# Attention and ternary feed-forward in float32 on one core: the feed-forward joins the block of projections and attention

## What is computed

```python
x = x + attention(layernorm(x))       # causal; q, k from latents, half of each head rotated
x = x + ffn(layernorm(x))

def ternary_quant(w):
    scale = mean(abs(w)) + 1e-8
    return clip(round(w / scale), -1, 1) * scale

up, gate = h @ wu.T, h @ wg.T          # 512 -> 2048
hidden = silu(up) * gate
return hidden @ wd.T                   # 2048 -> 512
```

## Time and profile before

| | |
|---|---|
| time, median of 3 runs | 1896.14 us (1895.67 to 1896.91) |
| the profiled execution | 1895.38 us, span 1893.6 us, mean TensorE clock 0.992 |
| TensorE (PE) busy | 1834.3 us, 97%, 10898 matmuls |
| VectorE (DVE) busy | 1337.8 us, 71% |
| ScalarE (ACT) busy | 1036.3 us, 55% |
| GpSimd (POOL) busy | 521.9 us, 28% |
| DMA | 153.31 MB, mean 81 GB/s |

### The profile page before, as it was taken

One profiled execution on the slowest core, in us unless ns is written; L12 is line 12 of the kernel. 1 busy time (PEld: TensorE's weight loads), 2 busy tenths in 40 slices (PEclk: granted clock), 3 DMA queues, 4 the chain that ended last, 5 costly groups with the idle time before them and its releaser, 6 DMA issues. The chain is left out here.

```text
span 1893.6 us, 30946 instructions
## 1 busy us (share of the span) xinstructions
PE 1834.3 (97%) x10898; PEld 1602.4 (85%) x10898; DVE 1337.8 (71%) x2818; ACT 1036.3 (55%) x2485; POOL 521.9 (28%) x314
## 2 busy tenths in 40 slices
PE   6899988999999999999999999999999799999998
PEld 4788876899999999999999999999999677777777
DVE  5466657888888888888888888888888633333333
ACT  2223326786777766676666666676666332223232
POOL 4466652120120154253244235234323000000000
PEclk9999999999999999999999999999999899999999
DMA  3399996422232121221221221212111150000000
GB/s 120 113 226 226 224 234 176 129 73 77 65 94 62 50 80 62 62 62 62 68 62 62 58 65 52 73 40 68 40 57 39 58 210 1 22 0 22 15 7 22
DMA packets 96625, 153.31 MB, mean 81 GB/s; under 512 B 12528, under 2 KB 46448, under 8 KB 96240
## 3 DMA queue, kind: packets, MB, share of 16 engines
q1 hardware_dynamic: 84976, 130.66, 23.5%
q10 hardware_dynamic: 11520, 20.98, 4.2%
HBM read 97.06 MB, written 54.53 MB: 80 GB/s over the span
## 5 line engine op out<-in xcount | busy, mean ns | idle before, releaser
L1140 ACT CAST turned_hi<-ps_turn 128x512 fp32r<-128x512 f32 (+1 forms) x576 | 312.8, 570 | 257.2 <-PE ps_turn L1325 253.3
L1096 ACT ACTIVATE probs<-ps_scores,bias 128x512 f32<-128x512 f32 (+3 forms) x640 | 401.0, 639 | 71.1 <-DVE bias L1184 70.9
L1223 DVE TENSOR_TENSOR turned_lo<-ps_turn,turned_hi 128x512 fp32r<-128x512 f32 (+1 forms) x576 | 375.0, 656 | 60.7 <-ACT turned_hi L1140 55.4
L1325 PE MATMUL ps_turn<-ident,probs 128*128 128x128 f32 x2176 | 300.9, 272 | 1.4 <-DVE turned_lo L1223 1.1
L1181 DVE TENSOR_REDUCE negmax<-ps_scores 128x1 f32<-128x512 f32 (+1 forms) x384 | 257.4, 675 | 44.9 <-PE ps_scores L1284 39.6
L1325 PEld LDWEIGHTS ps_turn<-ident,probs 128*128 128x128 f32 x2176 | 255.4, 140 | 33.5 <-issue 2.2
L1026 POOL TENSOR_TENSOR q_lo<-q_raw,q_hi 128x512 fp32r<-128x512 f32 x64 | 82.8, 1294 | 677.0 <-ACT q_hi L1088 677.0
L1284 PE MATMUL ps_scores<-k_hi,q_hi 128*128 128x512 f32 (+2 forms) x576 | 231.0, 401 | 4.5 <-ACT probs L1096 4.4
L1344 PE MATMUL ps_o<-turned_hi,kv_hi 128*128 128x256 f32 x1088 | 226.7, 285 | 0.0
L1344 PE MATMUL ps_o<-turned_lo,kv_hi 128*128 128x256 f32 x1088 | 223.6, 282 | 0.0
L1344 PE MATMUL ps_o<-turned_hi,kv_lo 128*128 128x256 f32 x1088 | 223.4, 282 | 0.0
(11 more groups left out here) (152 smaller groups left out, 3502.8 us busy)
## 6 DMA issues: line engine op xcount, KB each, us to landing
plainT<-plain_out ACTq DMA_DIRECT2D x64, 256.0 KB, 4.0
rotT<-rot_out SPq DMA_DIRECT2D x64, 256.0 KB, 4.3
all_signs<-signs SPq DMA_DIRECT2D x24, 512.0 KB, 2.8
q_raw<-plainT SPq DMA_DIRECT2D x128, 64.0 KB, 2.4
q_raw<-rotT SPq DMA_DIRECT2D x256, 32.0 KB, 2.1
signs<-in_W_up SPq DMA_DIRECT2D x16, 512.0 KB, 3.6
signs<-in_W_gate SPq DMA_DIRECT2D x16, 512.0 KB, 3.7
signs<-in_W_down SPq DMA_DIRECT2D x16, 512.0 KB, 3.6
```

The source lines that it names most:

```text
L1096: nc.scalar.activation(probs_of(n, i)[:, h, first_key:first_key + keys], ps_scores[:, pieces.number[args] % RING, 0:keys], ACT.Exp, scale= ...
L1140: nc.scalar.copy(turned[0][:, at, cols(*args)], ps_turn[:, bank, cols(*args)]).then_inc(turned_hi_ready, 1)
L1223: nc.vector.tensor_tensor(turned[1][:, at, cols(*args)], ps_turn[:, bank, cols(*args)], turned[0][:, at, cols(*args)].bitcast(F32), ALU.su ...
L1325: last = nc.tensor.transpose(ps_turn[:, bank, (2 * b + h) * P:(2 * b + h + 1) * P], probs_of(n, i)[:, h, key:key + P], ident[:])
```

## The change

One block now holds projections, attention and feed-forward; `feed_forward` gives each engine's part as functions. Its code is written out, with no loop: 64 steps over (chunk, step), `down` a step late across chunks, up two steps ahead at the start, and no normalising in the last chunk. Its buffers lie over those that the attention has done with (`places`), its PSUM banks are ps_scores (up, gate, turns) and ps_turn and ps_o (sums). y holds the tiles in the order of the slots (15, 0, 14, 1, ...), so that the first chunk of the feed-forward is complete after two slots of the last pass; x is loaded tile by tile, 16 DMAs in place of 4.

In the last pass `Plan` has new events: the statistics at steps 40 to 49, the root at 64, normalising, transposes and splits of the first chunk from 64.4 on, and the weights' loads at 55 (4 tiles) and 66 (11 tiles; 9 more follow in the feed-forward). Behind the last pass up and gate of the first steps lie between the last output products.

In `last_order` the EARLY stages lie one piece later or earlier; the key splits go head by head, those of the second head's low parts to GpSimd.

```diff
@@ last_order @@
-    order += [(EARLY, 1), (ROT, 0, 1), (EARLY, 2), (PLAIN, 0, 0), (PLAIN, 0, 1), (EARLY, 3)]
-    order += [(ROT, 1, 1), (EARLY, 4), (PLAIN, 1, 0), (PLAIN, 1, 1)]
-    order += [(ROT, 2, 1), (PLAIN, 2, 0), (PLAIN, 2, 1), (EARLY, 5)]
-    return order + [(ROT, 3, 1), (PLAIN, 3, 0), (PLAIN, 3, 1)]
+    order += [(EARLY, 1), (ROT, 0, 1), (PLAIN, 0, 0), (PLAIN, 0, 1), (EARLY, 2)]
+    order += [(ROT, 1, 1), (PLAIN, 1, 0), (PLAIN, 1, 1), (EARLY, 3)]
+    order += [(ROT, 2, 1), (PLAIN, 2, 0), (PLAIN, 2, 1), (EARLY, 4)]
+    return order + [(ROT, 3, 1), (PLAIN, 3, 0), (PLAIN, 3, 1), (EARLY, 5)]
@@ Plan @@
-        self.only[0] += [(12, 0, "load_y", (2,)), (16, 0, "load_y", (1,))]
+        self.only[0] += [(4 + 12 * m, 0, "load_y", (m + 1,)) for m in range(NC - 1)]
...
+        last += [(40 + 3 * t, 0, "ln_stats", (t,)) for t in range(TC)] + [(53, 0, "ln_var", ()), (64, 0, "ln_root", ())]
...
+        last += [(55, 0, "load_ffn", (0,)), (66, 0, "load_ffn", (1,))]
...
@@ early_scalar @@
+        if stage == 2:
+
+            split_hi(act, 0, "split_q", (0,), 0)
             act.wait_ge(first_loaded, 48)
...
+            first_high(act, 0, 0)
+            first_high(act, 0, 1)
         if stage == 3:
...
+            for h, c in ((0, 2), (0, 3), (1, 0), (1, 1)):
+                first_high(act, h, c)
+        if stage == 4:
+            first_high(act, 1, 2)
+            first_high(act, 1, 3)
             split_hi(act, 0, "split_q", (1,), 0)
@@ early_gpsimd @@
+        if stage == 2:
+            split_lo(pool, 0, "split_q", (0,), 1)
+        if stage == 3:
+            low(1, 0)
+        if stage == 4:
+            low(1, 1)
+            low(1, 2)
+            low(1, 3)
+        if stage == 5:
+            split_lo(pool, 0, "split_q", (1,), 2)
@@ early_vector @@
-        if stage in (2, 4):
-            for c in (stage - 2, stage - 1):
-                for h in range(2):
-                    raw, hi, lo = first_views(c, h)
-                    dve.wait_ge(first_hi_ready, 2 * c + h + 1)
-                    nc.vector.tensor_tensor(lo, raw, hi.bitcast(F32), ALU.subtract).then_inc(first_ready, 1)
...
+        if stage in (3, 4):
+            for c in (2 * stage - 6, 2 * stage - 5):
+                raw, hi, lo = first_low(dve, 0, c)
+                nc.vector.tensor_tensor(lo, raw, hi, ALU.subtract).then_inc(first_ready[0], 1)
@@ attention, tensor @@
+                if kind in TAIL:
+                    if (kind, *args) == ("h_turn", 0):
+
+                        pe.wait_ge(exp_done, RING + softened.upto(last_of_all, 0))
+                    tail["tensor"](pe, kind, *args)
@@ feed_forward @@
+    def tensor(pe):
+        down(pe, 0)
+        for n, i, e in steps():
+            if n > AHEAD:
+                into_hidden(pe, n, UP)
+            into_hidden(pe, n, GATE)
+            down(pe, n - 1)
+            if i + 1 < NC and e in NORM_AT:
+                turn(pe, i + 1, NORM_AT[e])
+        down(pe, NC * ET - 1)
```

More of the change, by code:

```diff
@@ L643 @@
 NSLOTS = len(SLOTS)
+TILES = [t for tiles in SLOTS for t in tiles]
 CHUNKS = len(MATS) * PAIRS
@@ new lines, in down @@
+    def down(pe, n):
+        i, e = divmod(n, ET)
+        pe.wait_ge(hid_lo_ready, n + 1)
+        for t in range(TC):
+            if e == 0 and i:
+                pe.wait_ge(result_ready, TC * (i - 1) + t + 1)
+            if n == 0 and t == TC - 1:
+                pe.wait_ge(*keep["outs_over"])
+            for part in range(2):
+                last = nc.tensor.matmul(ps_acc[t], hid[part][:, n % 2, t * P:(t + 1) * P],
+                                        wT[DOWN][e // 2][:, e % 2, :], start=(e == 0 and part == 0),
+                                        stop=(e == ET - 1 and part == 1))
+            if e == ET - 1:
+                last.then_inc(acc_ready, 1)
@@ new lines, in sync, with scalar @@
+    def sync(sp):
+        sp.wait_ge(gate_ready, AHEAD + 1)
+        for c in range(5, PAIRS):
+            for m in (UP, GATE, DOWN):
+                load_weights(sp, m, c)
+        for i in range(NC):
+            for t in range(TC):
+                sp.wait_ge(result_ready, TC * i + t + 1)
+                sp.dma_start(out.rearrange("(t p) d -> t p d", p=P)[TILES[TC * i + t], :, :],
+                             result[:, t, :]).then_inc(stored[t], 16)
+    def scalar(act):
+        for n, i, e in steps():
+            silu(act, n)
+            hidden_high(act, n)
+            if i + 1 < NC:
+                if e == ROOT_AT:
+                    root(act, i + 1)
+                if e in NORM_AT:
+                    h_high(act, i + 1, NORM_AT[e])
@@ L1751, in _ @@
                     att["tensor"](pe)
[L1752 removed]
+                    ffn["tensor"](pe)
 def by_unit(name, w):
```

490 lines of the change are left out of this document (250 added, 240 removed).

## The result

| | |
|---|---|
| after, median of 4 runs | 1862.47 us (1857.74 to 1865.71) |
| before, median of 4 runs beside it | 1895.91 us (1893.55 to 1896.91) |
| ratio | 0.9822, 95% interval 0.9808 to 0.9836 |
| profiled execution after | 1864.14 us, span 1862.3 us |
| forecast | 1872.0, range 1864.5 to 1880.0 |

The change is faster, as forecast, but by 33.4 us instead of 24. The profiled run itself was 31.2 us faster than the one of before.

A forecast was written before the change was run, and what follows sets the result against it. TensorE was taken to set the pace in the attention, with holes at two seams and feed-forward stalls. -4.4 + 0.5 + 2.1 + 2.3 - 18.1 - 4.2 - 1.8 = -23.6 from 1895.4 gave 1872 us, range 1864.5 to 1880.

The forecast's parts named there:

- First seam: Projections to attention: reordered key splits and scores start the first exponentials earlier, -4.4 us, bounds -7.5 and 0.
- The slip of 1.5 us: First seam: two plain stores running against the query loads delay the queries' landing by 0 to 2.1 us, taken as 1.5.
- The rival: First seam: the reorder gives nothing, from delayed queries and engines locking each other out; 1876, at most 1878 us; chance 0.12.
- The lock of VectorE and GpSimd: First seam: the engines fully block each other, two splits held up 1.15 us each; the part gives -2.1, not -4.4.
- Statistics, transposes, normalising in the last pass: Last attention pass: added statistics +0.5, 16 transposes +2.1, root and normalising of the first chunk +2.3 us.
- the dearer price of a switch: Last pass, ScalarE's root: table switch of 1.28 us plus a drain of 1.38 more, making the +2.3 part +3.7.
- The rival of VectorE as the bound: Last pass: 3.5 us of statistics and 4.9 of normalising both come through, 1879 us; chance 0.10.
- Second seam: Attention to feed-forward: up and gate fill the hole, 11.4 us against 29.5 from the last value product, -18.1 us.
- Feed-forward without a loop: Feed-forward: down a step late across chunks removes six stalls of 0.70 us, -4.2; turning no unused chunk, -1.8.
- the unused turns: Feed-forward: the loop's fourth round turned a following chunk for nobody; dropping its 16 transposes gives -1.8 us.
- My sign for "wrong": Feed-forward in the changed profile: starts more than 0.2335 us apart would show the forecast wrong.
- Slower because the written-out code isn't fed: Unrolled feed-forward: some 2,300 more instructions, 6 more instruction-queue packets at 5.0 us each, 30 us, 1902; chance 0.03.

The follow-up runs named there:

- e1: Kernel before with only the new order at the first seam (last_order, key and query splits, scores one piece earlier): 1892.12 us against 1895.15, ratio 0.9982.
- e5: Kernel before with 32 bytes of padding ahead of hT, leaving the feed-forward's operands 192 apart modulo 256: 1895.42 us, ratio 0.9994.
- e9: Kernel before with hT, hidden and result 96 bytes further, so feed-forward operands start at the same place modulo 256: 1885.24 us, ratio 0.9957.
- e10: Kernel before with hT, hidden and result 224 bytes further, operands 128 apart modulo 256: 1895.16 us, ratio 0.9997.
- e3: Kernel before with the feed-forward's PSUM banks placed as in the changed kernel, nothing else moved: 1897.63 us, ratio 1.0010.
- e2: Kernel before with only TensorE's feed-forward loop written out: 1896.06 us, ratio 1.0005.
- e6: Kernel before with wT moved 32 bytes further instead of hT, operands 192 apart modulo 256: 1895.66 us, ratio 0.9996.
- e13: Kernel before with all matmul operands padded to 128 modulo 256: 1882.53 us, ratio 0.9931.
- e12: Changed kernel with the last down product of each chunk back inside its chunk: 1865.00 us, ratio to before 0.9853.
- e8: Changed kernel with gated, hidden and its two parts 32 bytes further, so only the down product is out of step: 1863.42 us, ratio to before 0.9825.
- e14: Changed kernel with 96 bytes of padding ahead of all tiles behind the scales, all operands at 128 modulo 256: 1856.71 us, ratio to before 0.9800.

## Why the prediction was right or wrong

**First seam: right in size, not in shape.** -4.4 stood against -4.59 in the traces and -4.95 in the means. I had one hole of 6 us near 282, and the trace of the changed kernel has 1.94 and 1.29 and then two waits on VectorE's splits. The slip of 1.5 us that I gave the queries didn't come. They were there 10.89 us behind the last wvo product before and 10.05 after, 1.72 us after ScalarE was ready for them, and so the bank was free earlier than in my walk. The first exponentials gained more than I said (21.80 us behind the wvo product instead of 28.37), and 2 us of that were gone at the fifth output product. ScalarE's wait of 2.55 us for the second head's maxima lies between; that it took them is argued, not shown. The granted clock fell to 0.50 at this seam too, for 6.8 us before and 3.4 after, in the other profiles for 10.2 to 13.7 with the old order and 0 to 6.8 with the new; the walk had no price for it, and how much of the gain it is wasn't told apart. That the size came out is in part luck. The rival fell with e1 and the stretches beside it.

The lock of VectorE and GpSimd, which I had priced at 2.3 us, is there in full:

```profile
287.47 3.04 DVE L1235 TENSOR_TENSOR k_lo<-first_raw,k_hi 128x512 fp32r<-128x512 f32 x2 [3.79 <-ACT k_hi L1065]
...
292.75 0.92 DVE L1235 TENSOR_TENSOR k_lo<-first_raw,k_hi 128x512 fp32r<-128x512 f32 x1 [0.24 <-DVE by_sin L561]
293.59 1.77 DVE L1235 TENSOR_TENSOR k_last_lo<-first_raw,k_last_hi 128x512 fp32r<-128x512 f32 x1
```

and GpSimd beside it:

```profile
287.00 1.27 POOL L1049 TENSOR_TENSOR q_lo<-q_raw,q_hi 128x512 fp32r<-128x512 f32 x1 [4.85 <-ACT q_hi L1131]
288.65 1.31 POOL L506 TENSOR_TENSOR rot_out<-by_cos,by_sin 128x512 f32<-128x512 f32 x1 [0.38 <-POOLq L505]
...
293.08 1.74 POOL L506 TENSOR_TENSOR rot_out<-by_cos,by_sin 128x512 f32<-128x512 f32 x1
```

The second split ends at 290.51, 0.55 us behind the addition that GpSimd had begun before it (289.96), and k_last_lo at 295.36, 0.54 behind the next one (294.82). The other two do the same. In all 16 profiles the splits that are held up end 0.55 behind the GpSimd instruction that began first, and those beside an idle GpSimd take 0.68. Where both begin within 0.01 us, it can be GpSimd's that waits (e5, e9, e10). GpSimd's second addition in turn took 1.74 instead of 1.3, behind the split at 292.75. So each waits until the other is through. All four of the first head's splits were held up in the changed kernel, where the sum by the lock counted two, and four of eight before. Even so the part gave -4.6 to -4.95 and not -2.1: the walk had 1.0 to 1.5 us for a split already, and of TensorE's five holes two, 2.2 us together, ended on VectorE.

**Statistics, transposes, normalising in the last pass: right.** +0.5, +2.1 and +2.3 against +4.78. With the output products of the two traces laid beside each other, the changed kernel loses 0.1 us up to the statistics, 0.6 while they run, and 4.1 in the last 25 us or so, where 4.4 were forecast. How these 4.1 divide into transposes and waits was not tested. TensorE's stalls on the normalised tiles were 0.63 and 0.68, those on the additions 0.36 and 0.53. ScalarE's table load took 1.28 us and the root started 0.01 behind it, so the dearer price of a switch (+3.7 for this part) didn't come. The rival of VectorE as the bound (+7.1 more) had no place: between 310 and 1483 us TensorE waits for VectorE and ScalarE 1.3 us in all.

**Second seam: right against the trace that it was read from, 2 to 3 us low against most others.** -18.1. From the last value product to the first down product it is 29.76 before and 13.16 after, of which 1.82 are the extra up: -18.4. Of the nine profiles with the old seam only before and e5 have 29.76; seven have 31.9 to 33.1. The granted clock tells them apart (windows, columns as in rows 1), in the kernel before and in e3:

```profile
1502.20:1515.70 13.50, 5.20 (x19) 4.05 (x19) 8.53 (x20) 3.01 (x5) 0.00 (x0) 0.50 0.61 224
```

```profile
1498.40:1522.20 23.80, 12.93 (x35) 9.21 (x36) 11.76 (x26) 5.60 (x8) 0.00 (x0) 0.50 0.62 241
```

TensorE had been busy 2.69 of 5.70 us (1496.40 to 1502.10) when its clock fell to 0.50, the lower level of 1.2 GHz. It stayed there for 13.7 us in before and e5, for 20.5 in e1, e2, e6, e9 and e10 (31.9 to 32.1 us in all) and for 23.9 in e3 and e13 (33.1 and 32.9), so that in seven of nine the first feed-forward products ran at it too. No profile with the new seam has such a stretch here. So the seam is worth 18.4 us against the trace of before and some 20.5 to 21.7 against most; I read one trace, and priced the clock as it was in that one.

**The feed-forward: the step that failed.** In the part "Feed-forward without a loop" I took only stalls (-4.2, shown by e12 as 4.7) and the unused turns (-1.8) out and let every one of its 1536 matmuls keep "0.2335 us apart". I read that number from the trace as a property of the instruction. It is one of the pair of operands: they lay 160 bytes out of step modulo 256, and the change puts all tiles in new places, where they are in step. The term that I had at 0 was 1536 x 0.0065 = -10.0 us, and -9.9 is what the fourth stretch was off by. Both paces stood in the trace of before, 0.227 in the projections' later x products and 0.234 in their query products (the lines from 118.92 on); I never asked why two like matmuls differ. My sign for "wrong", starts more than 0.2335 apart, looked to one side alone.

That the place sets the pace is shown from both sides (e9 and e8). e13 with e14 says that nothing else of size was missed: their traces differ by 26.1 us; e14 started 3.7 later (89.0 against 85.3), and e13's second seam had 3.1 more than that of before (32.89 against 29.76). Without these two the difference is 26.6, and 3 us are left over my sum, 1.2 of them at the first seam. By what mechanism the place acts isn't known from these runs. Of the distances tried, 0 is fast, and in the feed-forward 32 (e8), 128, 160 and 192 bytes are 2.5 to 3% slower.

**Slower because the written-out code isn't fed: no.** The instruction queue moved 85 packets instead of 76, nine more rather than six, and TensorE waited 0.5 us in the whole feed-forward, for something else. e2, which writes out TensorE's loop and nothing else, moved the same 85, and its time is that of before within 0.14%.

**The range** held the price of each wait, and none for a quantity that I had taken as fixed. A bound on the pace from the nearest rows (0.2267, the other pace of the same trace) would have put its low end 10 us lower, and the measured 1862.5 inside.

## What to carry to other kernels

When a change moves buffers, the pace of every matmul that reads them is a term of the sum: compare like matmuls within one trace, and if two paces exist, print the operands' addresses modulo 256 before believing either (the matmuls just behind a slow kind are slow too, so compare those further on). Where they differ, a pad of some words ahead of one tile is worth trying first: 96 bytes gave 8 to 10 us here, about twice what the reordered first seam did. And time an edit against its rival in equal places (e13 and e14), since a layout that comes along by luck can be a quarter to a third of what the edit seems to bring. Where a term closes a hole, read the granted clock of the hole in more than one profile.

## What the runs showed of the hardware

- Two float32r operands at the same place modulo 256 give a 512-wide matmul every 0.2267 us, the others tried in the feed-forward every 0.2325 to 0.2335 (means of the stretch), and the projections' query products, 96 apart, every 0.234, at a granted clock of 1.00 in all, the higher of its levels. The Trainium skill (TensorE: Matmul & The Clock Gate, section "Wait — 56ns, not 53.3ns?") has 215.7 ns for a warm, back-to-back matmul of 512 columns; no stretch here reached that. The Trainium skill (SBUF — State Buffer, section Operand start alignment) says of its own measurements that they are "about legality, not speed"; here the start of an operand changed the speed.
- Behind transposes, a stall or products out of step, the first five to ten products run at the slow pace even when their operands are in step.
- A VectorE subtraction of two SBUF tiles that begins while GpSimd works on two SBUF tiles waits for its end: 0.68 us alone, 0.9 to 1.8 when held up, and then it ends 0.55 us behind the other, in all 16 profiles. GpSimd's waits in the same way (1.27 alone, 1.74 behind the split at 292.75).
- Between attention and feed-forward TensorE's granted clock fell to 0.50 (1.2 GHz) for 13.7, 20.5 or 23.9 us in the nine profiles with the old seam (in before, after 5.70 us of which it was busy 2.69). The same work took 29.8, 32 and 33 us by it. With the new seam, where TensorE is busy 12.22 of 13 us, the clock stayed at 1.00.
- The first wvo product of one and the same program came at 92.0 and 87.3 us, and over all profiles between 85.3 and 92.0. Between the two profiles of the changed kernel it is 4.65 of the 5.5 us by which their spans differ; whether it makes up the 8 us between the fastest and the slowest execution isn't shown, since those two have no profile.
